# Query and key stacks by way of a DRAM scratch, and projections moved to earlier units

## The chip, the cores and the metric

One NeuronCore of a Trainium2 chip runs the whole program. The metric is the device time of one execution in microseconds, as the median of several runs. Where a number comes from a trace, it comes from one profiled execution.

## What is computed

Four blocks on x of 2 x 512 tokens by 512 features, each as x + layernorm(block(layernorm(x))): a state-space mixer, a ternary feed-forward, an attention and a mixture of eight experts. The change lies in the third:

```python
q = (x @ Wq.T + bq).reshape(b, l, h, hd).transpose(0, 2, 1, 3)   # b=2, l=512, h=32, hd=16
k = (x @ Wk.T + bk).reshape(b, l, h, hd).transpose(0, 2, 1, 3)
v = (x @ Wv.T + bv).reshape(b, l, h, hd).transpose(0, 2, 1, 3)
scores = jnp.einsum('bhqd,bhkd->bhqk', q, k) / math.sqrt(hd)
att = jax.nn.softmax(jnp.where(causal, scores, -jnp.inf), axis=-1)
out = jnp.einsum('bhqk,bhkd->bhqd', att, v).transpose(0, 2, 1, 3).reshape(b, l, d)
return out @ Wo.T + bo
```

## The kernel before

TensorE multiplies in a rounded 32-bit type (F32R). To keep full precision each operand is split in a high part and a low part (what the rounding lost), and `products` adds high x high, high x low and low x high.

**Passes, quads, units.** Attention runs over 8 passes m = 0..7: four tiles t of 128 features (8 heads each) times two batches. `project` (L1849) makes 128 features of the queries (w = 0), then of the keys (w = 1), for 512 tokens of one batch, in bank 7; each in four parts of three matmuls. ScalarE's `high` (L1141) casts the result into `qh`, VectorE's `lows` (L1480) writes the rest into `ql`, and then bank 7 is free for the next. A pass has two quads of four heads. A quad has 8 units (`unit`, L431): for each 128 queries qi = 0..3 two head pairs p2. Two units have the same qi, and a unit's width grows with qi. A pass m so covers units 16m to 16m+15, and all engines walk the units in order.

**A unit.** TensorE makes the scores of a head pair (L1896) and adds the mask (L1897); VectorE takes the negated maximum (L1492); ScalarE the exponentials into `prob` (L1173); two units later TensorE transposes them (L1907), and ScalarE and VectorE copy them into `pA` or `pB` (L1165, L1501). The value products `weighted(quad, 0)` run in the quad's unit 6, `weighted(quad, 1)` in unit 2 of the next, its output's transposes (L1918) in unit 4 (`A_AHEAD`, `B_AHEAD`, `O_BACK`). `pieces` (L448) says after which units the parts of the next pass's projections run: 3 to 6 of the 16 for the queries, 8 to 11 for the keys.

**The stacks.** The scores take all parts in one matmul with the parts one above the other on partitions: `qs` holds for a pair of heads three blocks of 32 rows (query high, low, high) and 32 zero rows; `kz` holds (key high, high, low), for each of the two heads j apart, with zeros in the other's rows. `qs` and `kz` have two buffers, by quad. SyncE's queue fills them from `qh` and `ql` by SBUF-to-SBUF transfers: for each quad 6 into `qs` (64 KB each, L590) and 12 into `kz` (32 KB each, L595), 18 in all. Before a pass's first stack it waits for the scores of the quad two before (L583) and for `lows`; TensorE waits for all 18 at each quad's first unit (L1891). `high` of the next pass waits until the stacks are filled from `qh` (L1146). After pass m = 0, 2, 4, SyncE loads the next tile's weights `aqr`; ScalarE's `weights` scales and casts them after unit 14 (L1181) and GpSimd makes their low parts (L890).

**Before attention.** The third norm's tiles come one after the other; TensorE's loop (L1843) transposes tile i and makes the values of tile i-2 (12 matmuls); after the loop it projects queries and keys of pass 0, with `high` and `lows` after each, and SyncE fills the first stacks. ScalarE casts `wo` into `awh` when all value products are made (L1136 to L1139), GpSimd makes its low part, and ScalarE starts on the units only then (L1155), since the raw weights lie where `prob` does.

Of the kernel before, what the change touches and what calls it, by code (L numbers as in the profile page):

```python
# [14 lines left out]
P = 128  # L15
# [20 lines left out]
VW = HD + 1  # L36

# [20 lines left out]
def program(nc, hidden, w_conv, w_gate, w_dt, conv_w, conv_b, dt_bias, A_log, Dskip, norm_w, w_out,  # L58
            ff_gu, ff_dn, gate_s, up_s, down_s, wq, wk, bqk, wv, bv, wo, bo, gate_w, expert_w, out):
    ctx = ExitStack()  # L60
    with ctx:
# [230 lines left out]
        qk_in = [sem(f"qk_in{n}") for n in range(2)]  # L292
        s_ready, max_ready, exp_ready, pt_ps, pt_a, pt_v, pv_ps, o_out, o_tr, prec_ready, att_ready = (sem(s) for s in (
# [18 lines left out]
        yd = nc.dram_tensor("yd", (PAIRS + SLOT_TILES * P, DM), F32).ap()  # L312

# [159 lines left out]
        STACK = 2 * (3 + 3 * 2)  # L473

        def stacked(quad):

            return 16 * STACK * (quad // 2 + 1)

# [16 lines left out]
        def _(sp):  # L495
# [72 lines left out]
            if STAGES >= 3:  # L568
# [10 lines left out]
                for m in range(AT * NB):  # L579
                    for u in range(2):  # L580
# [3 lines left out]
                        for w in range(2):  # L584
                            sp.wait_ge(qk_l, 2 * m + w + 1)
                            for p2 in range(2):
                                of = 32 * (2 * u + p2)
                                for r, part in enumerate((qh, ql, qh) if w == 0 else (qh, qh, ql)):
                                    if w == 0:
                                        sp.dma_start(qs[32 * r:32 * r + 32, quad % 2, p2, :].bitcast(F32), part[of:of + 32, w, :].bitcast(F32)  # L590
                                                     ).then_inc(qk_in[quad % 2], 16)
                                    else:
                                        for j in range(2):
                                            row, at = of + HD * j, 32 * r + HD * j
                                            sp.dma_start(kz[at:at + HD, quad % 2, p2, j, :].bitcast(F32), part[row:row + HD, w, :].bitcast(F32)  # L595
                                                         ).then_inc(qk_in[quad % 2], 16)
# [140 lines left out]
        def _(pool):  # L737
# [140 lines left out]
            if STAGES >= 3:  # L878
# [4 lines left out]
                pool.memset(qs[3 * 32:P, :, :, :].bitcast(F32), 0.0).then_inc(sel_ready, 1)  # L883
# [1180 lines left out]
```

## Time and profile before

| | |
|---|---|
| median of 3 runs | 1714.3 us (1713.21 to 1725.72) |
| the profiled execution | 1710.41 us |
| its span, first to last instruction | 1708.7 us |
| attention's units in it, first scores to last copy | about 1231 to 1524 us |
| TensorE busy | 1535.8 us (90%) |
| VectorE, ScalarE, GpSimd busy | 1198.4, 809.2, 835.6 us |
| granted TensorE clock, mean | 0.96 |

The median is what is predicted. The profiled execution is a single one, with its own time; durations and starts are taken from it. An engine's busy share says little by itself: the span is set by the chain of work in which each step is released by the one before.

### The profile page before, as it was taken

The page shows a single profiled execution, that of the slowest core. Times are in us where ns is not written, and L with a number is a line of the kernel's source. Part 1 is how long each engine was busy: PE and PEld are TensorE (multiplying, and loading weights), DVE is VectorE, ACT ScalarE, POOL GpSimd, SP SyncE. Part 2 cuts the span into 40 slices and gives each one's busy share as a digit, 9 for nine tenths or more (in the row PEclk, how much of TensorE's full clock was granted, in tenths as well). Part 3 has the DMA queues.
Part 4 walks back from the last instruction along what each step waited for, and adds up shares of the span by engine and source line. Part 5 has one row for each costly group of instructions (what it writes and reads, how often), then busy time and mean ns, then how long its engine had stood idle before and what let it go on. Part 6 is the DMA issues. An engine that isn't in the chain of part 4 may idle for free.

```text
span 1708.7 us, 26177 instructions
## 1 busy us (share of the span) xinstructions
PE 1535.8 (90%) x8646; PEld 1197.6 (70%) x8646; DVE 1198.4 (70%) x2000; ACT 809.2 (47%) x1604; POOL 835.6 (49%) x761
## 2 busy tenths in 40 slices
PE   5899999999999999999999869996688888887796
PEld 3677877878778778777787658875565655666583
DVE  5777887788788787887787865657366666668524
ACT  3455555555545555555554423341266656564130
POOL 4377586676675766776766840007200000018454
PEclk9999999999999999999999889997899999997798
DMA  3111012021110110211101122120122111242344
GB/s 120 37 50 63 13 51 67 11 84 33 47 58 18 49 61 12 80 37 49 61 19 50 57 56 74 62 98 25 33 54 55 42 52 45 51 180 74 113 140 178
DMA packets 60249, 105.19 MB, mean 62 GB/s; under 512 B 12624, under 2 KB 37328, under 8 KB 54928
## 3 DMA queue, kind: packets, MB, share of 16 engines
q1 hardware_dynamic: 56496, 92.19, 17.5%
q0 software_dynamic: 3680, 12.06, 2.1%
q8 instruction: 42, 0.69, 0.2%
q14 instruction: 31, 0.25, 0.0%
HBM read 81.14 MB, written 10.49 MB: 54 GB/s over the span
## 4 chain that ended last, share of the span: by engine, by line
PE 57%; DVE 15%; POOL 8%; issue 7%; ACT 6%; DMA 4%; SPq 3%; POOLq 0%; DVEq 0%; ACTq 0%
PE banks L365 28%; PE banks L1653 6%; DVE tap L1235 4%; SPq L595 3%; PE banks L1907 3%; PE banks L1790 3%; PE banks L1718 2%; PE banks L1712 2%; PE banks L1683 2%; DMA x<-in_w_gate 2%; POOL wol L370 2%; PE banks L1875 2%; PE banks L1727 2%; PE banks L1896 2%; DVE nmax L1492 1%
## 5 line engine op out<-in xcount | busy, mean ns | idle before, releaser
L1235 DVE SCALAR_TENSOR_TENSOR tap<-banks,parg,tap 128x511 f32<-128x511 f32 (+2 forms) x288 | 215.1, 747 | 26.4 <-ACT tap L949 19.2
L755 POOL TENSOR_TENSOR am<-ah,upto 128x1024 fp32r<-128x1024 f32 x64 | 121.7, 1901 | 177.6 <-PE banks L1683 136.5
L365 PE MATMUL banks<-xTh,wch 128*128 128x512 f32 x384 | 162.2, 422 | 5.4 <-DVE em L1341 4.9
L957 ACT ACTIVATE th<-tap 128x512 f32<-128x512 f32 x96 | 60.7, 632 | 213.0 <-DVE tap L1235 211.0
L365 PE MATMUL banks<-xTh,wcl 128*128 128x512 f32 x384 | 151.0, 393 | 0.0
L365 PE MATMUL banks<-xTl,wch 128*128 128x512 f32 x384 | 150.1, 391 | 0.0
L1173 ACT ACTIVATE prob<-banks,nmax 128x128 f32<-128x128 f32 (+3 forms) x256 | 122.0, 526 | 59.1 <-DVE nmax L1492 58.2
L1492 DVE TENSOR_REDUCE nmax<-banks 128x2 f32<-128x256 f32 (+3 forms) x128 | 105.0, 820 | 55.8 <-PE banks L1897 55.8
L1907 PE MATMUL banks<-ident,prob 128*128 128x128 f32 x640 | 106.8, 296 | 18.5 <-DVE pB L1501 8.6
L755 POOL TENSOR_TENSOR am<-al,upto 128x1024 fp32r<-128x1024 f32 x64 | 122.1, 1908 | 0.0
L1341 DVE TENSOR_TENSOR em<-banks,gmask 128x1024 f32<-128x1024 f32 x64 | 78.2, 1222 | 50.3 <-ACT banks L998 49.5
L1896 PE MATMUL banks<-kz,qs 128*128 128x256 f32 (+2 forms) x192 | 76.0, 436 | 37.8 <-DMA kz<-ql 34.6
L365 PE MATMUL banks<-xTh,wgh 128*128 128x512 f32 x256 | 107.4, 420 | 0.9 <-DVE tap L1235 0.5
L370 POOL TENSOR_TENSOR aql<-aqr,aqh 128x512 fp32r<-128x512 f32 x8 | 10.0, 1275 | 190.1 <-ACT aqh L1099 190.1
L365 PE MATMUL banks<-woh,ynTh 128*128 128x512 f32 x256 | 102.8, 402 | 0.0
L365 PE MATMUL banks<-woh,ynTl 128*128 128x512 f32 x256 | 101.0, 394 | 0.0
L365 PE MATMUL banks<-xTh,wgl 128*128 128x512 f32 x256 | 100.8, 394 | 0.0
L365 PE MATMUL banks<-wol,ynTh 128*128 128x512 f32 x256 | 100.7, 393 | 0.0
L365 PE MATMUL banks<-xTl,wgh 128*128 128x512 f32 x256 | 100.1, 391 | 0.0
L1907 PEld LDWEIGHTS banks<-ident,prob 128*128 128x128 f32 x640 | 78.4, 153 | 27.4 <-DVE pB L1501 12.5
L365 PEld LDWEIGHTS banks<-xTh,wch 128*128 128x128 f32 x384 | 72.1, 188 | 34.1 <-DVE em L1341 11.2
L1653 PE MATMUL banks<-xTh,gu 128*128 128x512 f32 x224 | 89.9, 401 | 6.1 <-DVE hidf L1430 6.1
(284 smaller groups left out, 4245.6 us busy)
## 6 DMA issues: line engine op xcount, KB each, us to landing
x<-grownT SPq DMA_DIRECT2D x96, 128.0 KB, 4.7
x<-in_w_conv SPq DMA_DIRECT2D x7, 1536.0 KB, 6.6
x<-in_w_gate SPq DMA_DIRECT2D x8, 1024.0 KB, 5.0
x<-in_w_out SPq DMA_DIRECT2D x8, 1024.0 KB, 4.8
eraw<-in_expert_w SPq DMA_DIRECT2D x8, 1024.0 KB, 7.3
gur<-in_ff_gu SPq DMA_DIRECT2D x7, 1024.0 KB, 4.8
x<-in_hidden SPq DMA_DIRECT2D x16, 256.0 KB, 3.8
qs<-qh SPq DMA_DIRECT2D x64, 64.0 KB, 2.0
```

The lines of the kernel that those rows point to most:

```text
L365: m = nc.tensor.matmul(o, a, b, start=first and n == 0, stop=last and n == len(terms) - 1)
L595: sp.dma_start(kz[at:at + HD, quad % 2, p2, j, :].bitcast(F32), part[row:row + HD, w, :].bitcast(F32)).then_inc(qk_in[quad % 2], 16)
L755: m = pool.tensor_tensor(am[:, part, :, :], a[:, i, :].bitcast(F32).unsqueeze(2).to_broadcast([P, HG, P]), upto[:, :].unsqueeze(1).to_broa ...
L957: nc.scalar.activation(th[:, :], tap[:, q % 2, :], ACT.Tanh).then_inc(tanh_ready, 1)
L1173: e = nc.scalar.activation(prob[:, n % 2, j, 0:kw], scores(n)[:, j, :], ACT.Exp, bias=nmax[:, n % 2, j:j + 1])
L1235: nc.vector.scalar_tensor_tensor(tap[:, q % 2, sh:L], bk(CONV_BANKS[q % 2])[:, 0:L - sh], parg[:, KC * q + k:KC * q + k + 1], tap[:, q % 2 ...
L1341: nc.vector.tensor_tensor(em[:, s % 2, :, :], decayed, gmask[:, :].unsqueeze(1).to_broadcast([P, HG, P]), ALU.mult).then_inc(m_ready, 1)
L1492: nc.vector.tensor_reduce(nmax[:, n % 2, :], scores(n), AX, ALU.max, negate=True).then_inc(max_ready, 1)
L1653: m = mat(bk(2 * w + ft), gu[:, k, ft, w, :], part[:, k, tok], start=(k == 0 and part is xTh), stop=(k == KT - 1 and part is xTl))
L1790: m = mat(bk(4 + i % 4), part[:, k, i * P:(i + 1) * P], dn[:, k, :], start=(k == 0 and part is hidh), stop=(k == 1 and part is hidl))
L1896: mat(o, qs[:, quad % 2, p2, qi * P:kw], kz[:, quad % 2, p2, heads[0]:heads[1], 0:kw], start=True, stop=False)
L1907: m = pe.transpose(bk(4 + j)[:, c * P:(c + 1) * P], prob[:, w % 2, j, c * P:(c + 1) * P], ident[:, :])
```

## The change

1. A DRAM tensor `stacks` takes, for each pass, queries and keys, head by head: four parts of 16 rows by 512 tokens. For w = 0 these are high, low, high, low; for w = 1 high, high, low, low. Four stores of 256 KB for the queries, four for the keys, as soon as `lows` has made the low parts.
2. From there each quad's `qs` comes in one load (512 KB: the heads a of a pair, parts and rows on 128 partitions, both pairs), and `kz` in two (256 KB each, 64 partitions). Per quad 7 transfers instead of 18. The new semaphores `qk_out` count the stores; the loads wait for them, and so does `high` of the next pass. With four parts there are no zero rows in `qs`, and GpSimd's memset of them goes.
3. The projections of the next pass run after units 0 to 3 (queries) and 4 to 7 (keys). ScalarE casts the next tile's weights, and GpSimd makes their low parts, after unit 9 instead of 14.
4. The projections of pass 0 move into the values loop, two parts after each of the steps i = 5 to 8, and `high` and `lows` of pass 0 move between the norm's steps.

```diff
@@ pieces
-            for w, at in ((0, (3, 4, 5, 6)), (1, (8, 9, 10, 11))):
+            for w, at in ((0, (0, 1, 2, 3)), (1, (4, 5, 6, 7))):
@@ 
-        STACK = 2 * (3 + 3 * 2)
         def stacked(quad):
-            return 16 * STACK * (quad // 2 + 1)
+            return 16 * 3 * (quad // 2 + 1)
@@ SyncE
                 for m in range(AT * NB):
+                    for w in range(2):
+                        sp.wait_ge(qk_l, 2 * m + w + 1)
+                        for r, part in enumerate(((qh, ql, qh, ql), (qh, qh, ql, ql))[w]):
+                            sp.dma_start(stacks[m, w, :, r, :, :], part[:, w, :].bitcast(F32)).then_inc(qk_out[w], 16)
+                    queries = stacks[m, 0].rearrange("(u p a) r d l -> u (a r d) p l", u=2, p=2)
+                    keys = stacks[m, 1].rearrange("(u p a) r d l -> u a (r d) p l", u=2, p=2)
                     for u in range(2):
                         quad = 2 * m + u
                         if quad >= 2:
                             sp.wait_ge(s_ready, 8 * (quad - 1))
-                        for w in range(2):
-                            sp.wait_ge(qk_l, 2 * m + w + 1)
-                            for p2 in range(2):
...
-                                        sp.dma_start(qs[32 * r:32 * r + 32, quad % 2, p2, :].bitcast(F32), part[of:of + 32, w, :].bitcast(F32)
-                                                     ).then_inc(qk_in[quad % 2], 16)
...
+                        sp.wait_ge(qk_out[0], 16 * PARTS * (m + 1))
+                        sp.dma_start(qs[:, quad % 2, :, :].bitcast(F32), queries[u]).then_inc(qk_in[quad % 2], 16)
+                        sp.wait_ge(qk_out[1], 16 * PARTS * (m + 1))
+                        for j in range(2):
+                            sp.dma_start(kz[64 * j:64 * j + 64, quad % 2, :, j, :].bitcast(F32), keys[u, j]).then_inc(qk_in[quad % 2], 16)
@@ GpSimd
-                pool.memset(qs[3 * 32:P, :, :, :].bitcast(F32), 0.0).then_inc(sel_ready, 1)
-                pool.wait_ge(sel_ready, SEL + 3)
...
-                    if n % 32 == 14 and n // 32 + 1 < AT:
+                    if n % 32 == 9 and n // 32 + 1 < AT:
@@ ScalarE
-                norm_scalar(2)
+                def high(m, w):
+                    act.wait_ge(qk_ps, 2 * m + w + 1)
+                    at_least(act, qk_out[w], 16 * PARTS * m)
...
+                act.wait_ge(small_in, 16 * 12)
...
+                for i in range(NT):
+                    norm_high(2, i)
+                    if i >= NT - 2:
+                        high(0, i - NT + 2)
                 act.wait_ge(v_ps, NT)
                 act.wait_ge(awr_in, 32)
...
-                for w in range(2):
-                    high(0, w)
...
-                        if n % 32 == 14 and n // 32 + 1 < AT:
+                        if n % 32 == 9 and n // 32 + 1 < AT:
                             weights(n // 32 + 1)
@@ VectorE
-                norm_vector(2, 3, lambda n: values(n - 6) if n >= 6 else None)
+                def between(n):
+                    if n >= 6:
+                        values(n - 6)
+                    if n == NT + 2:
+                        lows(0, 0)
+                norm_vector(2, 3, between)
+                lows(0, 1)
                 for i in range(NT - 2, NT):
                     values(i)
@@ TensorE
                 for i in range(NT + 2):
                     if i < NT:
                         norm_turn(2, i)
                     if i >= 2:
                         values(i - 2)
+                    if CH + 1 <= i <= NT:
+                        if i == CH + 1:
+                            pe.wait_ge(down_added, 4 + NT * FP)
+                        for part in (0, 1):
+                            project(0, (i - CH - 1) // 2, 2 * ((i - CH - 1) % 2) + part)
...
-                for w in range(2):
-                    for part in range(KT):
-                        project(0, w, part)
                 pe.wait_ge(v_f, NT)
-                pe.wait_ge(sel_ready, SEL + 3)
+                pe.wait_ge(sel_ready, SEL + 2)
```

## Rows read from the trace of the kernel before

**Rows 1.** The page, chain that ended last: shares of the span by line

```profile
PE banks L365 28%; PE banks L1653 6%; DVE tap L1235 4%; SPq L595 3%; PE banks L1907 3%; PE banks L1790 3%; PE banks L1718 2%; PE banks L1712 2%; PE banks L1683 2%; DMA x<-in_w_gate 2%; POOL wol L370 2%; PE banks L1875 2%; PE banks L1727 2%; PE banks L1896 2%; DVE nmax L1492 1%
```

**Rows 2.** Waits, 1225:1520: who waited, for whom, us in total, times, longest

```profile
PE banks L1896 <- DMA kz<-ql: 34.6, 8, 10.5
```

**Rows 3.** Chain from 1290 to 1306: start us, duration us, what

```profile
1294.41 0.51 SPq L595
...
1300.02 1.51 SPq L595
...
1302.21 2.00 DMA kz<-ql
...
1304.25 0.39 PE banks L1896
```

**Rows 4.** Chain, products `weighted(quad, 1)`, slots 10, 2, 10, and of pass 7

```profile
1250.22 1.65 PE banks L1875 x32
...
1271.61 1.65 PE banks L1875 x32
...
1288.51 1.65 PE banks L1875 x32
...
1494.28 1.69 PE banks L1875 x32
...
1508.12 1.70 PE banks L1875 x32
```

**Rows 5.** Timelines: start us, duration, engine, line [idle before <-releaser], of VectorE, TensorE

```profile
1279.23 1.23 DVE L1492 TENSOR_REDUCE nmax<-banks 128x2 f32<-128x1024 f32 x1 [0.51 <-PE banks L1897]
...
1283.04 1.22 DVE L1492 TENSOR_REDUCE nmax<-banks 128x2 f32<-128x1024 f32 x1
...
1299.70 1.23 DVE L1492 TENSOR_REDUCE nmax<-banks 128x2 f32<-128x1024 f32 x1 [0.65 <-PE banks L1897]
...
1502.80 1.23 DVE L1492 TENSOR_REDUCE nmax<-banks 128x2 f32<-128x1024 f32 x1 [0.65 <-PE banks L1897]
...
1504.40 0.41 DVE L1492 TENSOR_REDUCE nmax<-banks 128x2 f32<-128x256 f32 x1
...
1516.63 1.22 DVE L1492 TENSOR_REDUCE nmax<-banks 128x2 f32<-128x1024 f32 x1 [0.64 <-PE banks L1897]
...
1295.64 0.44 PE L1907 MATMUL banks<-ident,prob 128*128 128x128 f32 x2 [1.10 <-DVE pA L1501]
...
1503.17 0.36 PE L1896 MATMUL banks<-kz,qs 128*128 128x256 f32 x1
```

**Rows 6.** DMA issues: out<-in, queue, kind, count, KB each, us to landing

```profile
aqr<-in_wq SPq DMA_DIRECT2D x4, 256.0 KB, 3.2
...
xnd<-acc SPq DMA_DIRECT2D x8, 256.0 KB, 2.0
```

**Rows 7.** Stretches: from:to, length, busy PE, PEld, DVE, ACT, POOL; clock, DMA, GB/s

```profile
1506.00:1508.00 2.00, 1.84 (x12) 1.29 (x12) 1.30 (x3) 1.65 (x6) 0.00 (x0) 1.00 0.99 418
...
1489.00:1521.00 32.00, 29.61 (x248) 20.58 (x248) 22.28 (x40) 21.75 (x50) 0.00 (x0) 0.95 0.50 189
```

**Rows 8.** Timeline of ScalarE, the next tile's weights after unit 14 of pass 0

```profile
1261.48 0.63 ACT L1096 ACTIVATE aqr<-aqr 128x512 f32<-128x512 f32 x1
1262.14 1.14 ACT L1099 CAST aqh<-aqr 128x512 fp32r<-128x512 f32 x2
```

**Rows 9.** Timelines ahead of the first scores: ScalarE, GpSimd, TensorE, VectorE

```profile
1213.33 2.18 ACT L1139 CAST awh<-prob 128x512 fp32r<-128x512 f32 x4 [7.82 <-PE banks L365]
...
1214.10 5.00 POOL L370 TENSOR_TENSOR awl<-prob,awh 128x512 fp32r<-128x512 f32 x4 [10.46 <-ACT awh L1139]
...
1217.68 0.51 PE L365 MATMUL banks<-xTh,aqh 128*128 128x512 f32 x1 [1.62 <-DVE ql L1483]
...
1221.49 0.75 DVE L1483 SCALAR_TENSOR_TENSOR ql<-banks,abqk,qh 128x512 fp32r<-128x512 f32 x1 [3.86 <-ACT qh L1147]
...
1231.22 0.55 PE L1896 MATMUL banks<-kz,qs 128*128 128x256 f32 x1 [10.49 <-DMA kz<-ql]
```

More of the change, by code:

```diff
@@ L36 @@
 VW = HD + 1
+PARTS = 4
 NE = 8
@@ L292, in program @@
         qk_in = [sem(f"qk_in{n}") for n in range(2)]
+        qk_out = [sem(f"qk_out{w}") for w in range(2)]
         s_ready, max_ready, exp_ready, pt_ps, pt_a, pt_v, pv_ps, o_out, o_tr, prec_ready, att_ready = (sem(s) for s in (
@@ L1134, in _ @@
             if STAGES >= 3:
-                norm_scalar(2)
-                act.wait_ge(v_ps, NT)
-                act.wait_ge(awr_in, 32)
-                for k in range(KT):
-                    nc.scalar.copy(awh[:, k, :], awr[:, k, :]).then_inc(aw_hi, 1)
                 def high(m, w):
                     act.wait_ge(qk_ps, 2 * m + w + 1)
-                    if m:
-                        for u in range(2):
-                            act.wait_ge(qk_in[u], stacked(2 * (m - 1) + u))
+                    at_least(act, qk_out[w], 16 * PARTS * m)
                     nc.scalar.activation(qh[:, w, :], bk(7), ACT.Identity,
@@ L1152, in _ @@
                 act.wait_ge(q_scaled, 2)
-                for w in range(2):
-                    high(0, w)
+                for i in range(NT):
+                    norm_high(2, i)
+                    if i >= NT - 2:
+                        high(0, i - NT + 2)
+                act.wait_ge(v_ps, NT)
+                act.wait_ge(awr_in, 32)
+                for k in range(KT):
+                    nc.scalar.copy(awh[:, k, :], awr[:, k, :]).then_inc(aw_hi, 1)
                 act.wait_ge(aw_lo, 2 * KT)
@@ L1473, in values @@
                                             abv[:, :].rearrange("p (h d) -> p h d", h=AH), ALU.add).then_inc(v_f, 1)
-                norm_vector(2, 3, lambda n: values(n - 6) if n >= 6 else None)
-                for i in range(NT - 2, NT):
-                    values(i)
-            if STAGES >= 3:
                 def lows(m, w):
@@ L1484, in lows @@
                                                    qh[:, w, :].bitcast(F32), ALU.add, ALU.subtract).then_inc(qk_l, 1)
-                for w in range(2):
-                    lows(0, w)
+                def between(n):
[5 more added lines that the diff above has]
+                lows(0, 1)
+                for i in range(NT - 2, NT):
+                    values(i)
+            if STAGES >= 3:
                 for n in range(UNITS + O_BACK - 7):
@@ L1839, in values @@
                                              for k in range(KT)]).then_inc(v_ps, 1)
-                pe.wait_ge(aw_lo, KT)
-                pe.wait_ge(hid_f, 4 * FP)
-                for i in range(NT + 2):
-                    if i < NT:
-                        norm_turn(2, i)
-                    if i >= 2:
-                        values(i - 2)
                 def project(m, w, part):
@@ L1861, in project @@
                         o.then_inc(qk_ps, 1)
+                pe.wait_ge(aw_lo, KT)
+                pe.wait_ge(hid_f, 4 * FP)
+                for i in range(NT + 2):
+                    if i < NT:
+                        norm_turn(2, i)
+                    if i >= 2:
+                        values(i - 2)
+                    if CH + 1 <= i <= NT:
[3 more added lines that the diff above has]
+                            project(0, (i - CH - 1) // 2, 2 * ((i - CH - 1) % 2) + part)
                 def weighted(quad, hf):
```

11 lines of the change are left out of this document (1 added, 10 removed).

## Prediction, written before the changed kernel was run

> **What bounds the kernel now.** I read the page first. Its chain that ended last is mostly TensorE's lines, but 3% of the span lie at line 595, a transfer issue on SyncE's queue [rows 1]. A DMA issue on such a chain means that an engine starves, so next I asked who waits for whom in the attention stretch (1225 to 1520 us): TensorE sat idle 34.6 us before line 1896, the scores, in 8 waits for the stack `kz`, the longest 10.5 us [rows 2]. Eight is the number of passes m, so the stall is one per pass. The chain at one of them shows its making: SyncE issues the first of twelve `kz` transfers at 1294.41 us, when the low key parts are there, and the twelfth at 1302.21, a pitch of 0.63 (one took 0.9 more), 2.00 us more until it lands, and the scores start at 1304.25 [rows 3]. SyncE's issue rate, not bandwidth, sets this: a transfer of 32 KB costs as much queue time as a large one.
>
> I call unit 16m+s "slot s" of pass m; slots 0-7 are one group of four heads, 8-15 the second. The value products `weighted(quad, 1)` run in slots 2 and 10, so their starts on the chain, some 17 us apart, are a clock; [rows 4] has the five I use. Slot 2 to slot 10 takes 16.90 us (1271.61 to 1288.51), with six projection parts in it and no stall. The last pass has no projections: 1494.28 to 1508.12, 13.84 us. So six parts and one `lows` cost 3.06. The seven stretches slot 10 to next slot 2 take 244.06 (1250.22 to 1494.28) less six of 16.90, 142.66 us, 20.38 each.
>
> What would a stretch be without its stall? In pass 1, just ahead of the stall of [rows 3], from slot 10's product at 1288.51 to the maximum of slot 15 at 1299.70 is 11.19; in the last pass the same is 1508.12 to 1516.63, 8.51 [rows 4, 5]. The 2.68 between is two projection parts, and the bubble that `lows` of slot 11 leaves (TensorE idles 1.10 us at 1295.64 for the vector copy of `pA` after it [rows 5]). A free stretch is thus 13.84 + 2.68 = 16.52, and a stall costs 20.38 - 16.52 = 3.86, 27.0 in seven. The waits alone are (34.6 - 10.5) / 7 = 3.44 each; 0.4 is the slow restart after them. The eighth stall, the longest, is the first stack.
>
> **The change part by part.**
> (1) *Stacks through DRAM.* 18 issues per four heads become 7: 4 stores and 3 loads. Now the path per pass. From the end of the low key parts: four stores of 256 KB. The trace has no SBUF-to-DRAM stores back to back; the nearest are `xnd<-acc`, of this size and direction: landing 2.0 [rows 6]. Bandwidth is 418 GB/s where 1 MB loads queue up [rows 7], so 1 MB of stores needs 2.5 us of data. The last store lands at 3 x 0.63 + 2.0 = 3.9 to 2.5 + 2.0 = 4.5. Then two `kz` loads of 256 KB, the second 0.6 later, landing 3.2 as `aqr<-in_wq` of that size does [rows 6], possibly behind the 512 KB query load (1.2 of data): 4.5 + 0.6 + 3.2 + 1.2 = 9.5, or 7.7 at best. If the stores serialise completely, 4 x 2.0, it is 13.0; I take 9, nearest to the row with queued loads.
>
> (2) *Projections sooner.* The key parts end in slot 7 instead of slot 11. What is the window? At slot 6 `lows` stands between two maxima, so that the second starts 3.81 after the first (1279.23 to 1283.04 [rows 5]); `lows` of slot 7 would end likewise 3.8 after slot 7's maximum, in the last pass's timing at 1502.80 + 3.81 = 1506.6. The scores of slot 16 would start 13.84 after those of slot 8 (1503.17), at 1517.0 [rows 5]. If TensorE makes up the whole delay by then, the window is 10.4 us; if none of it (the maximum of slot 8 at 1506.6 instead of 1504.40), 12.6. Against a path of 9 it is hidden, by 1.4 to 3.6. The other two waits in SyncE's order are no nearer: the first group's stack also waits for scores of slot 7, already made; the second group's waits for slot 15 of the pass before and is needed 8 slots later, with three loads (about 5 us) instead of 18. Query stores go out at slot 3. `high` waits for stores of a pass ago. Expected: all seven stalls gone, -27.0.
>
> (3) *What the moved parts cost where they land.* Slots 0-7 now hold all eight. Slots 4 to 6 keep theirs; 0 and 1 take those of 8 and 9, and 2 and 3 with a `lows` those of 10 and 11, slots of equal width and neighbours. New is that the key part in slot 4 needs bank 7 emptied by `lows` of slot 3 at once, with no slot between. After the `lows` of slot 11 TensorE idles 1.10 anyway for the vector copy [rows 5], and the part can fill this bubble. From below: if the bubble is filled whole, -1.1 per pass; from above, +1.0 per pass (the wait plus the delayed scores). I take -0.5 x 7 = -3.5.
>
> (4) *Weights at slot 9 instead of 14.* ScalarE's 0.63 and 1.14 [rows 8] used to lie in the stall. Now they stand between exponentials of light slots; the `pA` copy and the next exponential queue behind them, and transposes and scores wait for those. ScalarE is busy 21.75 of 32 us in the last pass [rows 7], so a third of its time can take them up: of 1.8 us I let 0.5 show. Three times: +1.5 (0 to 5.4). GpSimd's low parts then have 7 slots until they are needed, before 5; nothing.
>
> (5) *The first projections.* Before, the order is values, query part, a wait of 1.62, key part, and the low key parts from 1221.49 to 1222.24; then twelve issues, and scores at 1231.22, 9.0 later [rows 9]. Now one values tile (12 matmuls, as the key part from 1217.68 to 1220.6: 2.8) comes after the key part and the wait is covered by a values tile: `ql` ends 2.8 + 1.6 = 4.4 sooner, 1217.8, plus a path of 9: 1226.8, -4.4 (7.7 and 9.5 give -5.7 and -3.9). The wait that comes in its place: the cast of `wo` waits for all value products (1213.33 before); these now end 2.8 for the query part and 2.8 for the key part later, some 5.9 with gaps. ScalarE's first exponential waits for `wo`'s low part, which ended at 1219.10 [rows 9], so 1225.0 now: ahead of 1226.8 and no loss, but the gain can't pass 6. The projection parts go in after tile 4's transposes and are TensorE's own work either way.
>
> (6) *Removed*: the `qs` memset (GpSimd idles 10.46 before its next work [rows 9]) and the wait on it: 0. Expert loads start some 10 us sooner relative to attention; the exponentials and casts behind them wait for attention's end: 0.
>
> **Sum.** -27.0 - 3.5 + 1.5 - 4.4 = -33.4. I take off 2 for partial stalls where a window is short (for instance the pass in which the `wq`, `wk` loads share the queue): -31.4. The profiled execution took 1710.41 us (span 1708.7): 1679. The median of the runs is 3.9 above it, 1714.3: 1683.
>
> **Half the store rate.** The Trainium skill, page DMA: Bandwidth & Descriptors, section on why a DMA increments its semaphore by 16, says that a queue uses the largest number of engines up to 16 that divides the slowest dimension on both sides. On the DRAM side of each store that dimension is 8, so by the rule 8 engines would work; no row of before shows such a pattern. It is the mechanism of the first rival.
>
> **The rivals.**
> *A, stalls stay in part.* Half the queued rate, about 215 GB/s, makes the four stores 4.9 of data, landing at 6.9, and the path 6.9 + 0.6 + 3.2 + 1.2 = 11.9, in the midst of a window of 10.4 to 12.6: with 0.4 of stall and 0.4 of restart in seven and 2.9 at the start, 1683 + 8.5 = 1691. At 13 (stores one after another) 1.5 and 0.4 in seven and 4 at the start give 1683 + 17 = 1700. For it speaks that no row shows four such stores in a row, against it that no load of before is that slow. Chance 0.16.
> *B, the packing costs.* TensorE is 93% busy in the last pass [rows 7]; with the eight parts in one group it could lose 1.0 per pass in (3), the whole 5.4 in (4): 1683 + 10.5 + 3.9 = 1697. The even 3.06 for six parts speaks against it. Chance 0.10.
> *C, the other side: the DRAM trip is longer than what it replaces.* The place is the four stores and the loads that read them back. It decides at a path of 12.6 + 3.9 = 16.5 us, where a stall costs what it did; the twelve issues needed only 9.8, though starting four slots later. At 22, as if each of the seven transfers took 3 us by itself, 5.5 more in seven, 8.6 at the start (22 less 4.4 and 9.0) and -2.0 from (3) and (4) give 1714 + 45 = 1759. The 2.0 of `xnd` speaks against it. Chance 0.05.
> *D, no effect*, because something else ends the wait at slot 0 (SyncE's wait on the scores of slot 7, say): 1714. The chain in [rows 3], which goes from the issues straight into the scores, leaves it 0.03.
> The forecast keeps 0.66, with a range of its own of 1674 to 1692 (two of its seven waits kept would add 7.7).
>
> **Numbers.** Likeliest 1683. Low end: bubble filled (-4.2 more), weights free (-1.5), start at its 6 (-1.6), no deduction (-2): 1674; the high end takes in B and most of A, 1699. A measurement of this kernel tells about 1% (17 us) from no change. Faster by over 1% (below 1697): the forecast, most of B and two thirds of A, 0.85; within 1%: 0.10; slower: 0.05.
>
> **What would show it.** Right: TensorE's idle before the scores for `kz` is one wait of some 6 us instead of 34.6 in eight; slot 10 to slot 2 takes 15 to 16 us; last store's landing 4 to 5 us after `ql`; `kz` landing some 9 after. Wrong in (1): waits for `kz` remain seven. Wrong in (3): those are gone, yet the half-passes with parts take over 18 us. Wrong in (5): the first scores wait for ScalarE or come after 1228.

## The result, and the profile after

| kernel | median, us | lowest to highest | ratio to before, 95% interval |
|---|---|---|---|
| before | 1714.46 | 1713.21 to 1725.72 | |
| after | 1702.47 | 1700.98 to 1704.59 | 0.993 (0.9907 to 0.9952) |

The change makes the kernel 0.7% faster: 12.0 us, within the 1% that was called "no change". The forecast was 1683, with a range up to 1699; the measured time lies above it. The profiled execution took 1700.98 us, with a span of 1699.2 against 1708.7.

The view of who waited for whom, of the kernel after, for TensorE in the attention stretch (us in total, times, longest), answers [rows 2]:

```profile
PE banks L1900 <- DMA kz<-stacks: 29.2, 8, 12.7
...
PE banks L369 <- DVE ql L1475: 5.2, 7, 1.1
```

All seven stalls that were to go are still there, shorter. With the first stack's, which was to stay, 34.6 us became 29.2. The first is longer than before (12.7 against 10.5), the other seven have 16.5 us together, 2.4 each instead of 3.4. A second row is new: the projections (L369, the helper `products`) wait in each of seven passes for the low parts `ql`, 0.74 us on average.

The chain of the kernel after at the third pass's start (start us, duration us, what) answers [rows 3]:

```profile
1285.28 0.76 DVE ql L1475
...
1288.02 7.11 DMA stacks<-ql
1295.15 0.62 SPq L596
1295.81 4.36 DMA kz<-stacks
1300.22 0.39 PE banks L1900
```

Read it as two legs. From the end of the low parts at 1286.04 to the last store's landing at 1295.13 are 9.1 us; the fourth store alone takes 7.11 from its issue. From there two loads of `kz`, 0.66 and 4.36, are 5.0 us. Together 14.2 to the scores. The prediction had at most 4.5 and 5.0 for the two, and took 9 for the sum. The whole surprise is in the first leg.

And the same at the first stack, where the prediction wanted 9 us from `ql` to the scores and the trace has 14.0:

```profile
1217.52 0.76 DVE ql L1475
...
1220.25 7.11 DMA stacks<-ql
...
1228.04 4.09 DMA kz<-stacks
...
1232.26 0.55 PE banks L1900
```

**Where the 9.5 us of span come from.** Take three points in both traces: the first scores, the first scores of pass 7, the end. Up to the first scores the kernel after is 1.0 later (1232.26 against 1231.22), of which 0.8 arose before attention, where the code is the same. From there to the first scores of pass 7 it takes 246.1 instead of 257.8, which is 11.7 less. Behind that it loses 1.1. So the seven passes give all there is, and the start gives nothing.

### The profile page after: what moved, and what is told of

Read it like the earlier page. It is cut to its first block, busy times and chain, and to the rows that moved or that the text cites. A ratio compares the mean times of both kernels' runs of the same rounds, so it can differ in the third digit from the quotient of the medians.

```text
span 1699.2 us, 26000 instructions
## 1 busy us (share of the span) xinstructions
PE 1534.8 (90%) x8646; PEld 1194.0 (70%) x8646; DVE 1197.9 (70%) x2000; ACT 807.0 (47%) x1604; POOL 834.0 (49%) x760
## 4 chain that ended last, share of the span: by engine, by line
PE 54%; DVE 14%; POOL 8%; DMA 8%; issue 7%; ACT 6%; SPq 1%; POOLq 0%; DVEq 0%; ACTq 0%
PE banks L369 27%; PE banks L1656 6%; DVE tap L1232 4%; DMA stacks<-ql 3%; PE banks L1793 3%; PE banks L1686 2%; PE banks L1721 2%; PE banks L1715 2%; DMA x<-in_w_gate 2%; DMA kz<-stacks 2%; POOL wol L374 2%; PE banks L1911 2%; PE banks L1730 1%; DVE xbc L1238 1%; PE banks L1900 1%
## 5 line engine op out<-in xcount | busy, mean ns | idle before, releaser
L369 PE MATMUL banks<-xTh,wch 128*128 128x512 f32 x384 | 162.4, 423 | 4.7 <-DVE em L1338 4.2
L369 PE MATMUL banks<-xTh,wcl 128*128 128x512 f32 x384 | 150.9, 393 | 0.0
L369 PE MATMUL banks<-xTl,wch 128*128 128x512 f32 x384 | 150.2, 391 | 0.0
L1911 PE MATMUL banks<-ident,prob 128*128 128x128 f32 x640 | 100.7, 283 | 12.6 <-DVE pB L1504 6.4
L369 PE MATMUL banks<-xTh,wgh 128*128 128x512 f32 x256 | 107.5, 420 | 0.9 <-DVE tap L1232 0.5
L369 PE MATMUL banks<-woh,ynTh 128*128 128x512 f32 x256 | 102.7, 401 | 0.0
L1900 PE MATMUL banks<-kz,qs 128*128 128x256 f32 (+2 forms) x192 | 74.5, 428 | 30.6 <-DMA kz<-stacks 29.2
L369 PE MATMUL banks<-woh,ynTl 128*128 128x512 f32 x256 | 101.2, 395 | 0.0
L369 PE MATMUL banks<-xTh,wgl 128*128 128x512 f32 x256 | 100.8, 394 | 0.0
L369 PE MATMUL banks<-wol,ynTh 128*128 128x512 f32 x256 | 100.7, 394 | 0.0
L369 PE MATMUL banks<-xTl,wgh 128*128 128x512 f32 x256 | 100.1, 391 | 0.0
L369 PEld LDWEIGHTS banks<-xTh,wch 128*128 128x128 f32 x384 | 72.2, 188 | 33.5 <-DVE em L1338 10.5
L947 ACT ACTIVATE tap<-banks,parg 128x512 f32<-128x512 f32 x96 | 74.1, 772 | 41.4 <-PE banks L369 35.8
```

The costliest lines, as they stand in the source:

```text
L369: m = nc.tensor.matmul(o, a, b, start=first and n == 0, stop=last and n == len(terms) - 1)
L947: nc.scalar.activation(tap[:, q % 2, :], bk(CONV_BANKS[q % 2]), ACT.Identity, bias=parg[:, CT * KC + q:CT * KC + q + 1], scale=parg[:, KC ...
L1900: mat(o, qs[:, quad % 2, p2, qi * P:kw], kz[:, quad % 2, p2, heads[0]:heads[1], 0:kw], start=True, stop=False)
L1911: m = pe.transpose(bk(4 + j)[:, c * P:(c + 1) * P], prob[:, w % 2, j, c * P:(c + 1) * P], ident[:, :])
```

## The experiments

**What the stores' shape does.** In the kernel after, a store's side in DRAM is 8 heads of 16 rows, the heads four parts apart. The experiment puts the four parts inside each row of a head: the same bytes, the same four stores and three loads, but all 128 rows now lie at one equal pitch.

```diff
-        stacks = nc.dram_tensor("stacks", (AT * NB, 2, HT, PARTS, HD, L), F32).ap()
+        stacks = nc.dram_tensor("stacks", (AT * NB, 2, HT, HD, PARTS, L), F32).ap()
-   sp.dma_start(stacks[m, w, :, r, :, :], part[:, w, :]...)
+   sp.dma_start(stacks[m, w, :, :, r, :].rearrange("h d l -> (h d) l"), part[:, w, :]...)
-   queries = stacks[m, 0].rearrange("(u p a) r d l -> u (a r d) p l", u=2, p=2)
-   keys = stacks[m, 1].rearrange("(u p a) r d l -> u a (r d) p l", u=2, p=2)
+   queries = stacks[m, 0].rearrange("(u p a) d r l -> u (a d r) p l", u=2, p=2)
+   keys = stacks[m, 1].rearrange("(u p a) d r l -> u a (d r) p l", u=2, p=2)
```

> The changed kernel with one thing altered: the scratch is laid out (head, feature, part, token), so the 128 rows of a store have one uniform stride in DRAM and its slowest dimension is 128 instead of 8; the stacks' rows are permuted alike in queries and keys. Same 14 transfers per pass, same bytes. Theory 1 (half of the 16 DMA engines work on a store, as the DMA busy share of 0.45 to 0.61 at 143 to 207 GB/s says): the last store lands 4 to 5 us after the low key parts instead of 9.1, the path to the first scores is about 9 instead of 14.2, the seven waits for kz (16.5 us) vanish, the first scores of all come some 4 to 5 us sooner, and the time is 1676 to 1682. Theory 2 (a store to DRAM and its reading back are slow by themselves, whatever the pattern): the last store still lands about 7 us after its issue and the time stays at 1702.

Measured: 1681.33 us, ratio 0.9818 (0.9789 to 0.9848); 21.1 us faster than the kernel after. Its TensorE has one wait for `kz` left, the first. The view of waits of this experiment:

```profile
PE banks L1900 <- DMA kz<-stacks: 8.6, 1, 8.6
```

and its chain at the first stack:

```profile
1219.64 0.76 DVE ql L1475
...
1221.75 3.72 DMA stacks<-ql
...
1226.13 4.00 DMA kz<-stacks
1230.27 0.55 PE banks L1900
```

The last store lands 3.72 us after its issue instead of 7.11. The stretches of 1 us in which only query stores move data show why (from:to, length, busy PE, PEld, DVE, ACT, POOL, clock, mean busy share of the DMA engines, GB/s). First the kernel after:

```profile
1279.00:1280.00 1.00, 1.00 (x16) 0.74 (x18) 0.86 (x1) 0.95 (x3) 0.00 (x0) 1.00 0.61 203
1280.00:1281.00 1.00, 1.00 (x18) 0.67 (x11) 0.83 (x2) 0.60 (x2) 0.00 (x0) 1.00 0.54 188
1281.00:1282.00 1.00, 1.00 (x7) 0.53 (x7) 0.00 (x0) 0.66 (x2) 0.00 (x0) 1.00 0.48 143
1282.00:1283.00 1.00, 1.00 (x10) 0.96 (x9) 0.85 (x1) 0.48 (x1) 0.00 (x0) 1.00 0.53 199
```

and then the experiment, in the same columns:

```profile
1274.00:1275.00 1.00, 1.00 (x9) 0.92 (x8) 1.00 (x2) 0.77 (x3) 0.00 (x0) 1.00 1.08 365
1275.00:1276.00 1.00, 1.00 (x9) 0.57 (x8) 0.61 (x3) 0.72 (x2) 0.00 (x0) 1.00 1.06 330
```

Half the engines' time is used in the one, all of it in the other, at 183 and 348 GB/s on average. The packets of a whole set of four query stores differ as well (the view of DMA, of the kernel after and then of the experiment):

```profile
DMA packets 545, 1.07 MB, mean 120 GB/s; under 512 B 32, under 2 KB 32, under 8 KB 544
```

```profile
DMA packets 577, 1.07 MB, mean 194 GB/s; under 512 B 64, under 2 KB 64, under 8 KB 576
```

Both have 512 packets of 2 KB, the data, and one of another queue. Besides these there are 32 small packets, 8 for each store, in the kernel after, and 64, 16 for each store, in the experiment. This is the Trainium skill's rule (page DMA: Bandwidth & Descriptors, section on why a DMA increments its semaphore by 16 and not by 1), that a queue uses the largest number of engines up to 16 that divides the slowest dimension on both sides: 8 for a side of 8 heads, 16 for 128 rows. The trace agrees in the share, 0.48 to 0.61 against 1.06 to 1.08, and in the 8 and 16 small packets for each store; it doesn't show which engines work.

The issue itself is slower too. The line's own view, of the kernel after and then of the experiment (duration of an issue on SyncE's queue in ns, min/median/max):

```profile
L585 SPq DMA_DIRECT2D stacks<-qh x32: 570/586/704, 1209.5 to 1464.7; - x32
L585 SPq DMA_DIRECT2D stacks<-ql x32: 602/1010/1382, 1210.2 to 1466.0; - x32
```

```profile
L585 SPq DMA_DIRECT2D stacks<-qh x32: 319/385/464, 1211.6 to 1447.9; - x32
L585 SPq DMA_DIRECT2D stacks<-ql x32: 432/454/1228, 1212.0 to 1448.8; - x32
```

The 1.23 us is a single issue; all others of the experiment take 0.32 to 0.46.

**Is it the shape, or where the bytes lie?** The experiment above changed both: the place of each row in DRAM and the number of dimensions. First the rearrangement alone was taken out, so that the store is written with two dimensions again:

```diff
-   sp.dma_start(stacks[m, w, :, :, r, :].rearrange("h d l -> (h d) l"), part[:, w, :]...)
+   sp.dma_start(stacks[m, w, :, :, r, :], part[:, w, :]...)
```

> The kernel of e1_sixteen with the same layout, the same addresses and bytes, and only the store's access pattern written in three dimensions (8 heads, 16 features, 512 tokens) instead of two (128, 512). Theory 1a (the slowest dimension of the pattern sets how many DMA engines work): stores run at half busy share again and the last lands about 7 us after its issue: 1702, with seven waits for kz of some 2.4. Theory 1b (what was slow in the changed kernel is where its rows lie in DRAM): as e1_sixteen, 1681.

Measured: 1681.40 us, ratio 0.9825 (0.9803 to 0.9847), the time of the experiment before. The trace tells why: its record of the store's instruction has 128 rows of 2 KB in both kernels, where the kernel after has 16 by 8 such rows. Heads and rows at one common pitch were folded into one dimension anyway, so the two kernels do the same and this run says nothing on the question. Two more kernels made the difference real. Both write and read in the same way; the only difference is one unused row per head, which breaks the common pitch. (They load the queries in two transfers of 64 partitions instead of one, since the padding doesn't let 128 be written as one.)

```diff
-        stacks = nc.dram_tensor("stacks", (AT * NB, 2, HT, HD + 0, PARTS, L), F32).ap()
+        stacks = nc.dram_tensor("stacks", (AT * NB, 2, HT, HD + 1, PARTS, L), F32).ap()
```

Without the row:

> The same without the pad: e1_sixteen with four loads per quad instead of three. Both theories: one more issue of 0.63 ahead of the kz loads, in the shade of the stores' landing: 1681 to 1682.

With it:

> The uniform layout of e1_sixteen with one unused feature row (8 KB) after each head, so that the 128 rows of a store no longer have one stride and its slowest dimension must be the 8 heads; the stacks' query loads go by 64 partitions, so a quad has 4 loads instead of 3. To be read against e10_not_padded, which differs in the pad alone. Theory 1a (the pattern's slowest dimension sets the number of DMA engines): stores at half busy share, issue 0.6 instead of 0.4, the last landing 7 us after its issue, and 21 us slower than e10. Theory 1b (place in DRAM): as e10, within 2 us, since a pad of 8 KB hardly moves a row.

Measured: 1679.11 us without, ratio 0.9786 (0.9753 to 0.9819), and 1703.14 with it, ratio 0.9931 (0.9909 to 0.9954). 24.0 us for one unused row per head. In the trace's record the padded store is 16 by 8 rows again, the other 128. The padded kernel has the time of the kernel after, its stalls and its issue times; here are TensorE's wait of the padded kernel and its store line:

```profile
PE banks L1901 <- DMA kz<-stacks: 30.6, 8, 13.1
```

```profile
L585 SPq DMA_DIRECT2D stacks<-ql x32: 608/1010/1380, 1210.9 to 1469.7; - x32
```

and both of the one without padding:

```profile
PE banks L1901 <- DMA kz<-stacks: 8.7, 1, 8.7
```

```profile
L585 SPq DMA_DIRECT2D stacks<-ql x32: 432/452/460, 1210.6 to 1447.2; - x32
```

So the shape decides. The order of the bytes within a head doesn't: the padded kernel has the experiment's order and the slow time.

**Each half of the change alone.** The transfers as in the kernel after, and everything else as before (projections after units 3 to 6 and 8 to 11, the first ones after the values):

```diff
-            for w, at in ((0, (0, 1, 2, 3)), (1, (4, 5, 6, 7))):
+            for w, at in ((0, (3, 4, 5, 6)), (1, (8, 9, 10, 11))):
-                    if n % 32 == 9 and n // 32 + 1 < AT:
+                    if n % 32 == 14 and n // 32 + 1 < AT:
...
-                    if CH + 1 <= i <= NT:
...
-                            project(0, (i - CH - 1) // 2, 2 * ((i - CH - 1) % 2) + part)
+                for w in range(2):
+                    for part in range(KT):
+                        project(0, w, part)
```

> Only the transfers of the change: stacks through DRAM in the changed kernel's layout, but projections, the next weights and the first projections in the places of the kernel before. Both theories: the path from the low key parts to the scores grows from 9.8 to about 14.2 us with the same start, so each of the eight waits grows by 4.4 us: 1714 + 35 = 1749, with waits for kz of about 65 us in 8.

The same with the stores of 128 rows:

> As the run before, with the uniform store layout. Theory 1: the path is about 9 us, 0.8 shorter than the eighteen issues' 9.8, so eight waits shrink by 0.8 each: about 1707. Theory 2: as with the changed layout, 1749.

And the other half, on the kernel before: 18 transfers within SBUF, with the places of the kernel after (the start is left as it was):

```diff
-            for w, at in ((0, (3, 4, 5, 6)), (1, (8, 9, 10, 11))):
+            for w, at in ((0, (0, 1, 2, 3)), (1, (4, 5, 6, 7))):
-                    if n % 32 == 14 and n // 32 + 1 < AT:
+                    if n % 32 == 9 and n // 32 + 1 < AT:
```

> Only the places: the kernel before with the parts of the next pass's projections after units 0 to 3 and 4 to 7 and the weights after unit 9; the 18 SBUF-to-SBUF transfers per quad stay, and so do the first projections. The stall before each pass would go, but the cast of the next queries after unit 3 must wait until the second quad's stack has been filled from the same buffer, 11.4 us of issues and 2 of landing after unit 0: TensorE then waits some 8 us at unit 4 for bank 7. 1714 + 7 x (8 - 3.9) = 1743. If this wait were not what it looks like, the time would be 1687 (seven stalls of 3.9 gone).

| kernel | median, us | ratio, 95% interval | TensorE's waits for `kz` |
|---|---|---|---|
| transfers only | 1755.35 | 1.0245 (1.0217 to 1.0272) | 72.5 in 8 |
| transfers only, 128 rows | 1724.29 | 1.0066 (1.0042 to 1.009) | 41.0 in 8 |
| places only | 1721.4 | 1.004 (1.0023 to 1.0056) | 10.5 in 1 |
| both, 128 rows | 1681.33 | 0.9818 (0.9789 to 0.9848) | 8.6 in 1 |

The view of waits of the first, and then of the one with 128 rows:

```profile
PE banks L1897 <- DMA kz<-stacks: 72.5, 8, 16.8
```

```profile
PE banks L1897 <- DMA kz<-stacks: 41.0, 8, 11.5
```

Neither half gains anything alone. The first came out 6 us above its expectation, its waits 7.5 longer than foreseen. The trip through DRAM is not shorter than the twelve issues that it replaces: with 128 rows it takes 10.4 us in one of the passes (`ql` ends at 1300.25, scores at 1310.65). The second kernel's expectation was worked out from 9; 1.4 more in eight stacks are 11 of the 17 us by which it was missed, and where the rest comes from is open. The trip's worth is that it needs `qh` and `ql` for a shorter time, and that it can be given a window. The third kernel shows the first of these. Its seven stalls for `kz` are gone by its earlier places, but its view of waits has another row in their stead:

```profile
PE banks L365 <- DVE ql L1483: 30.2, 8, 4.7
PE banks L1896 <- DMA kz<-ql: 10.5, 1, 10.5
```

and its chain at one of them reads:

```profile
1280.46 1.94 DMA kz<-ql
1282.51 0.70 ACT qh L1147
1283.23 0.76 DVE ql L1483
1284.03 1.65 PE banks L365 x3
```

That is: a stack's last transfer lands, only then may `high` overwrite `qh`, then `lows`, and only then is bank 7 free for a projection, at which TensorE stands. The stacks' transfers come straight from `qh` and `ql`, so these and bank 7 are held until the second quad's transfers are through, and the next pass's projections now come too soon for that. The wait was moved from `kz` to bank 7, 4.1 us in each of seven. That is half of what was expected, and so the kernel came out at 1721.4 where 1743 was expected. The DRAM copy releases both after four stores.

**The first projections.** The kernel with stores of 128 rows, with the projections of pass 0 back behind the values (the last part of the diff above alone):

> The kernel of e1_sixteen with the projections of pass 0 back behind the values loop (and their high and low parts too). It prices part 4 of the change where the stores are quick. If the sum of the forecast holds, the low key parts end 4.4 to 4.7 us later and so do the first scores: 1681 + 4.5 = 1685.8. If the wo cast that moved behind the interleaved projections had set the start, nothing is lost: 1681.

Measured: 1685.6 us, ratio 0.9841 (0.9827 to 0.9856), against 1681.40 for its like in the same session (the kernel that writes the stores with two dimensions). 4.2 us, as the prediction's step 5 had it.

**Bank 7's wait.** In the kernel with 128-row stores the key parts start one unit later, so that a unit lies between the queries' last part and the keys' first:

```diff
-            for w, at in ((0, (0, 1, 2, 3)), (1, (4, 5, 6, 7))):
+            for w, at in ((0, (0, 1, 2, 3)), (1, (5, 6, 7, 8))):
```

> The kernel of e1_sixteen with the key parts after units 5 to 8 instead of 4 to 7, so that TensorE need not wait for bank 7 right after the query parts (0.74 us in each of seven passes). If that wait is on the path: 1681 - 5 = 1676. If the stack's path of 9.8 us no longer fits in the shorter window (11.9 less 1.7), waits for kz of about 0.5 come back and it stays at 1681; if the bubble is only moved, 1681 as well, but with no waits for kz.

Measured: 1673.96 us, ratio 0.9773 (0.9757 to 0.9789), 7.4 less than 1681.40 in the same session. TensorE no longer waits for `ql` at the projections, and there is still no second wait for `kz`. Its view of waits, and its timelines of VectorE and TensorE:

```profile
PE banks L1900 <- DMA kz<-stacks: 8.5, 1, 8.5
PE banks L1911 <- DVE pA L1504: 7.9, 7, 1.2
```

```profile
1281.48 0.75 DVE L1475 SCALAR_TENSOR_TENSOR ql<-banks,abqk,qh 128x512 fp32r<-128x512 f32 x1 [0.98 <-ACT qh L1137]
...
1292.44 0.36 PE L1900 MATMUL banks<-kz,qs 128*128 128x256 f32 x1
```

The scores come 10.2 us after the low key parts, with no idle time before them. The path fits in that with next to nothing left: the last `kz` load was issued at 1287.93 and took 3.7.

Two things keep the 7.4 from being the price of the `ql` wait. In the profiled executions, from the first scores of all to the last, this kernel takes 250.4 us and the one it is compared with 255.3; its stretches from slot 2 to slot 10 are 18.2 instead of 18.9. That is 4.9, what the expectation had (5), and the rest of the 7.4 is outside attention or in the spread of the runs (1678.40 to 1686.81 for the kernel it is compared with). And the `ql` wait, 5.2 in seven, went, but a wait of the transposes for `pA` came, 7.9 in seven, as the kernel before has it (7.7), while their waits for `pB` fell from 13.1 to 8.8. So the gap's gain is shown; that it comes from this one wait is not.

**Three parts instead of four.** The kernel after also adds a low by low product, which the kernel before leaves out. This experiment leaves it out again: three stores of 256 KB instead of four, a query load of 96 rows (384 KB) and key loads of 48 (192 KB), and zero rows in `qs` as before.

```diff
-PARTS = 4
+PARTS = 3
-   for r, part in enumerate(((qh, ql, qh, ql), (qh, qh, ql, ql))[w]):
+   for r, part in enumerate(((qh, ql, qh), (qh, qh, ql))[w]):
+                pool.memset(qs[3 * 32:P, :, :, :].bitcast(F32), 0.0).then_inc(sel_ready, 1)
```

> The kernel of e1_sixteen with three parts instead of four (high, low, high against high, high, low; the product of the two low parts is left out as in the kernel before), and 32 zero rows set once by GpSimd. Six stores instead of eight, three quarters of the bytes. The path shortens by an issue of 0.45 and 256 KB of data, about 1 us; only the first stack is on the path, so 1680. Were bandwidth or the stores' number still on the path in each pass, 7 us more: 1673.

Measured: 1677.29 us, ratio 0.9793 (0.9775 to 0.981), 4.1 less than 1681.40, where 1 was expected. The one wait left for `kz` is 2.5 shorter than the 8.6 of the first experiment, by its view of waits:

```profile
PE banks L1902 <- DMA kz<-stacks: 6.1, 1, 6.1
```

From the first scores to the last it takes 255.1 us, as with four parts (255.3). So the passes gain nothing, as expected. The profiled executions differ by 1.7 us only, so the 4.1 of the medians is in part their spread.

Both together, the gap and three parts:

> e7_gap and e8_three_parts together: key parts after units 5 to 8, three parts in the stacks, uniform stores. The gap is worth 7 us, the shorter path 2.5 at the first stack: 1674 - 2.5 = 1671.5, with one wait for kz of 6 us. If the two gains were one and the same, 1674.

Measured: 1673.35 us, ratio 0.9756 (0.9726 to 0.9785). It is the lowest median, 29 us below the kernel after, but its interval overlaps that of the gap alone. Against 1679.11 for the 128-row kernel of the same session it is 5.8 better.

**How near is the window?** With three parts, the key parts moved three units later, to the places at which the path should stick out in every pass:

```diff
-            for w, at in ((0, (0, 1, 2, 3)), (1, (4, 5, 6, 7))):
+            for w, at in ((0, (0, 1, 2, 3)), (1, (7, 8, 9, 10))):
```

> As e11_gap_three with the key parts after units 7 to 10. It tests the window that the analysis uses: low key parts to the scores of slot 16. That window measured 11.9 us in the changed kernel (key parts after 4 to 7) and 10.2 in e7_gap (5 to 8); units 9 and 10 take about 4 us more of it, so it is 6.2, and the path with three parts is about 8.8: seven waits of 2.6 and some slow clock, 1671.5 + 20 = 1691. If the loss of the changed kernel had been the crowding of the first quad and not the window, spreading the parts would help and the time would be 1668 to 1672.

Measured: 1696.9 us, ratio 0.9893 (0.986 to 0.9926), 20 us above the three parts at their first places and 24 above those with the gap, from which its 1691 was worked out. But seven waits of 2.6 are not there. The view of waits, and then the chain at one of the stalls:

```profile
PE banks L1902 <- DMA kz<-stacks: 9.5, 6, 6.1
PE banks L1913 <- DVE pA L1506: 13.7, 14, 1.2
```

```profile
1288.98 0.76 DVE ql L1477
...
1290.59 2.81 DMA stacks<-ql
...
1293.78 3.04 DMA kz<-stacks
...
1296.87 0.38 PE banks L1902
```

The path was 7.1 us, where 8.8 was expected: the stores land 2.81 after the last issue and the `kz` loads 3.04 after theirs. Five stalls of 0.4 to 1.5 remain, 3.4 in all. So this size was wrong, and the other 16 us have another cause. The transposes wait 1 us for `pA` fourteen times. From slot 10's products to the next slot 2's the three stretches that hold ScalarE's casts of the next weights take 19.5 to 19.9 us, the other four 15.5 to 16.7, where the kernel with the earlier places takes 14.0. The casts stand after unit 9 and now wait for the key parts, which end after unit 10 (ScalarE waits 3.1 us for them in the first of the three). But the granted clock differs too. Here are the first of the three and the first of the four (columns as above):

```profile
1247.89:1267.36 19.47, 16.25 (x127) 11.42 (x126) 11.82 (x21) 12.45 (x29) 2.50 (x2) 0.91 0.45 122
...
1285.59:1301.26 15.67, 14.31 (x126) 10.09 (x126) 11.58 (x21) 10.88 (x26) 0.00 (x0) 1.00 0.61 169
```

TensorE is busy 1.9 us longer in the first for nearly the same matmuls, at a clock of 0.91 (the third of the three has 0.83, the other four 1.00). And of the stretches from slot 2 to slot 10 four have 0.91 and take 18.2, two have 1.00 and take 16.7. So a good part of the 16 us is lower clock: these four alone are 6. What lowered it, the wait for the casts or the crowding of these units, no run separates.

## Why the prediction was wrong, point by point

**What bounds the kernel** was right: one stall per pass for `kz`, at the scores. With the stores at the full rate and the rest of the change as it is, the stalls go and the time is 1681.33, 1.7 from the forecast. That it is so near is in part luck, as steps 3 and 4 below show.

**Step 1, the stores: the term that failed.** The prediction had the last store land 3.9 to 4.5 us after `ql`. It landed after 9.1; with a 128-row side after 5.1 (1220.40 to 1225.47), so that even for that shape the term was a little low. This one term is why seven stalls stayed and the kernel took 1702 instead of 1683. The prediction took the landing of `xnd<-acc` (one store of 128 rows by itself) and the bandwidth of loads [rows 6, 7], and both belong to another shape. It knew the rule that speaks against it, gave it rival A and a chance of 0.16, and priced A too low as well: 6.9 for the stores. That was 1 MB at half of 418 GB/s plus 2.0; the stores moved 183 GB/s, the issues cost up to 1.38 us instead of 0.63, and the last one landed 7.11 after its issue. What it called "nearest to the row with queued loads" was a choice for the row of a different pattern, against a rule that named exactly this one.

**The loads** were right: 5.0 forecast, 5.0 and 4.8 measured, though in other parts. The second `kz` load of a pass's first quad lands 3.8 to 4.7 us after its issue in both kernels, where 3.2 + 1.2 was forecast; the query load is about to land when it is issued. With three parts, where such a load has 192 KB instead of 256, it took 3.04 in the chain above.

**Step 2, the window.** Forecast 10.4 to 12.6. In the kernel after it is 11.9: the scores start at 1300.22 after 2.31 us of wait, so they could have at 1297.9, and `ql` ends at 1286.04. So a path of 14.2 must stick out by 2.3, and does. With stores of 128 rows it is hidden in every pass.

**What a stall costs.** The prediction had 0.4 on top of each wait for the slow restart. In the kernel after that varies. These two stretches go from slot 10's products to the next slot 2's (columns as above, the clock ahead of the last two):

```profile
1288.70:1304.60 15.90, 13.51 (x123) 9.53 (x122) 10.64 (x20) 10.13 (x23) 0.00 (x0) 1.00 0.76 224
...
1323.50:1341.70 18.20, 15.20 (x126) 10.91 (x125) 10.70 (x20) 11.43 (x27) 2.53 (x2) 0.91 0.58 169
```

In the first TensorE waited 2.31 us and went on at the full clock; in the second it waited 2.92 and the granted clock is 0.91, time at the lower level, 1.2 GHz, included. The second is 2.3 longer and 0.6 of it is wait. All seven stretches, in order of time:

| wait for `kz`, us | granted clock | length, us |
|---|---|---|
| 1.87 | 1.00 | 15.5 |
| 2.31 | 1.00 | 15.9 |
| 2.92 | 0.91 | 18.1 |
| 2.57 | 0.90 | 17.8 |
| 2.15 | 1.00 | 15.7 |
| 2.23 | 1.00 | 15.8 |
| 2.43 | 0.90 | 16.4 |

The last ends in pass 7, which has no parts. Against the 14.0 of a stretch without a stall (below; 13.8 for the last) a stall cost 1.5 to 1.9 us at the full clock and 2.6 to 4.1 with the lower one. The longer waits were the ones followed by the lower clock here, but in the padded kernel one of 2.19 was followed by 0.90 and one of 2.58 by 1.00. The seven took 115.3 us; with 128-row stores they take 97.8, 2.5 less each.

The kernel before paid for it too: of its seven stretches only one has a clock of 1.00, the others 0.84 to 0.92. Its last two stalls are both 3.00 us long; the stretch at 1.00 takes 18.7 and the other, at 0.91, 20.1. So the slow restart was worth about 1.3 in this pair, not 0.4.

**Steps 3 and 4, the moved parts.** The chain of the first experiment has `weighted(quad, 1)` of slots 10, 2, 10 and 2, in two passes:

```profile
1252.71 1.70 PE banks L1883 x32
...
1266.69 1.65 PE banks L1883 x32
...
1285.61 1.70 PE banks L1883 x32
...
1299.60 1.65 PE banks L1883 x32
```

18.92 from slot 2 to slot 10, with six parts and both `lows`, and 13.98 or 13.99 from slot 10 to slot 2, with the two query parts of slots 0 and 1: 32.9 for a pass, where the steps summed to 16.90 + 16.52 - 0.5 = 32.9. The first of the two short ones holds the casts of the weights, and is no longer than the other, so step 4's 1.5 us were not needed.

Only the sum came out. By the prediction's own sign, step 3 is wrong when the stalls are gone and the stretches with the parts take over 18 us, and they take 18.9, 2.0 more than the 16.90 of before. The other stretch was to take 15 to 16 and takes 14.0: the two parts of slots 0 and 1 cost next to nothing there, 0.15 over the 13.84 of the last pass, and the stall had a slow restart of about 1.3 where 0.4 was taken. The two errors, +2.0 and -2.5, leave just the -0.5 that step 3 took, and this is luck. Of the first, 0.7 goes when the gap is put in; the bank-7 wait that step 3 priced from -1.1 to +1.0 is there, 0.74 in each of seven. The prediction put "the part can fill this bubble" where the trace after shows a wait.

**Step 5, the start.** Before attention the traces drift: the transposes of the third norm's fifth tile, the same code in all, start at 1190.16 before, 1190.93 after and 1193.05 in the first experiment. Counted from there `ql` ends 4.7 us sooner in the kernel after and 4.7 in the experiment, where 4.4 were expected. The kernel after gave it all back by its path of 14.0; with 9.8 in the experiment, 3.8 stayed. The cover of `wo`'s cast held: the first scores waited for `kz`.

**The rivals.** A is what happened, in its mechanism; its price of 1691 to 1700 missed as above. B (the packing costs) fell with the 32.9. C, whose decisive path was 16.5, was nearer than its 0.05 says: the path was 14.2, and in the places of before the trip cost 40 us (1755.35 against 1715.75 for the kernel before in the same session). D fell with the first experiment.

## What to carry to other kernels

Before a DRAM scratch is priced, look at the outermost dimension that is left of each store once equal pitches are folded: 8 instead of 128 halved the rate here, and took away 21 of the 33 us that the change can be worth; another order of the dimensions costs nothing. A price taken from a transfer of the same size but another shape is no bound. And look at the granted clock of a stretch before its length is put down to a wait: here it was 1 to 2 us of a stretch of 16. And where a part is moved sooner, ask for how long its source is held: the earlier places took 39 us off with a copy that releases it (1724.29 to 1685.6), and cost 6 without (1721.4 against 1715.75).

## What the runs showed of the hardware

- A store of 256 KB with 8 as its slowest dimension in DRAM used half of the DMA engines' time (share 0.48 to 0.61, 143 to 203 GB/s), one with 128 rows all of it (1.06 to 1.08, 330 to 365 GB/s). One unused row per head makes the second into the first, 24 us. A set of four leaves 32 small packets beside the data in the first case and 64 in the second.
- SyncE's issue of a store of the first kind took 0.57 to 1.38 us, of the second 0.32 to 0.46, but for a single one of 1.23.
- Rows and heads at one common pitch, written as two dimensions, stood in the trace's record of the instruction as 128 rows, and took the same time as one dimension (1681.40 against 1681.33).
- The second of two loads of 256 KB, 0.6 to 0.7 us behind the first, landed 3.8 to 4.7 us after its issue, in the first quad of each pass, with a load of 512 KB just ahead of them.
- Stalls of TensorE of 1.9 to 2.9 us were followed by a granted clock of 1.00 in four stretches of the kernel after and of 0.90 to 0.91 in three; two stalls of 3.00 in the kernel before by 1.00 in one and 0.91 in the other, which took 1.3 us longer. Why the one and not the other, no run tells.
